# Gathering each 128-edge tile once a pass, with its visits reading a ring of tiles through registers

## The chip, the cores and the metric

One core of a Trainium2 chip runs the whole program. The metric is the device time of one execution in microseconds (us).

## The reference, cut to what matters

Three passes over the same 100,000 edges, sorted by destination node (6,250 nodes, 256 features). Each is an attention: a logit for each edge (and head), a softmax over the edges of a destination, and a weighted sum of the source rows.

```python
# layer 0, "gat": 4 heads of 64
logits = leaky_relu(a_src[src] + a_dst[dst], 0.2)
alpha  = segment_softmax(logits, dst)
x1     = segment_sum(h[src] * alpha[:, :, None], dst)
# layer 0, "attn": 1 head of 256
logits2 = einsum('ec,ec->e', q[d2], k[s2]) / sqrt(256)
out     = segment_sum(v[s2] * segment_softmax(logits2, d2)[:, None], d2)
# layer 1, "typed": 8 heads of 32, two edge types, a weight for each edge
alpha = leaky_relu(sum(xs_j * att_src[etype]) + sum(xd_i * att_dst[etype]))
out   = segment_sum(xs_j * (softmax over dst of alpha) * ew, dst)
```

Dense products, layer norms and a feed-forward stage stand between and behind the passes.

## The kernel before, in words

The edges lie in 782 tiles of 128. The nodes lie in 49 blocks of 128. A *visit* is one tile seen from one block: since edges are sorted, a tile that straddles two blocks has two visits, so there are at most 782 + 48 = 830 visits, padded to 832, in 52 batches of 16 (G). `edge_pass` runs once for each pass. Its engines each walk over the visits in a loop over v, and meet by semaphores alone:

- POOL (GpSimd, line 278) gathers the 128 source rows of a visit from a table in HBM by an indirect DMA, into one of 48 slots (gat, typed) or 40 (attn) of the ring X. It waits until the visit that had the slot is summed. The source numbers come from `tables`, which SP loads batch by batch; a tile with two visits is gathered twice.
- DVE (VectorE) makes the logits of a batch one batch ahead, at v = 16(k-1) for batch k. In gat and typed `source_logits` (line 466 or 469) adds the logit parts, which the gathered rows carry behind their 256 features, to those of the block. In attn `dot` (line 454) multiplies the gathered row with the expanded query, 25 visits ahead. A chain of scans (lines 515 to 566) takes the maxima of segments. Then `scale_rows` (line 591) multiplies each row by its weights in place, and `add` (line 613) adds the sum of the visit, which PE left in PSUM, to the block's accumulator. `blocks_of` (line 444) loads the 16 block numbers of a batch into DVE's registers.
- PE (TensorE) expands block values to edges (line 374 or 378), turns one-hot matrices (line 388), and sums a visit's rows by a matmul with the one-hot (line 425). `block_of` (line 356) loads four block numbers into PE's registers.
- ACT (ScalarE) copies the turned one-hots (line 334), takes exponentials (`weigh`, lines 287 to 299), in gat makes the transposed one-hots (lines 319, 326), in attn makes weighted one-hots (lines 307, 313).
- SP (SyncE) issues all other transfers of the pass (lines 227 to 250): tables, positions or one-hots, segments, joins, and in gat the stores of the one-hots.

```python
pool.wait_ge(S["summed"], v - RING + 1)                       # 277
pool.indirect_dma_start(X[:, v % RING, :], None, ph.table, ...)   # 278
row = X[:, v % RING, 0:D].rearrange("p (h c) -> p h c", h=H)
nc.vector.tensor_tensor(row, row, spread(row_weights[:, g, :], D // H), ALU.mult)   # 591
```

Of the kernel before, what the change touches and what calls it, by code (L numbers as in the profile page):

```python
# [23 lines left out]
PE_ENGINE = mybir.EngineType.PE  # L24

# [6 lines left out]
NT = (E + P - 1) // P  # L32
PAD_NODE = NP - 1
# [8 lines left out]
A = 6  # L42
SEG = 3 * P + 1
ARENA = 10400
BIG = 1e30
DST_SCALE = 1e30
FAR = 1000.0
H0, H2, FFN = 4, 8, 1024
W0 = D + 2 * H0
W1 = D + 4  # L50
# [81 lines left out]
class Phase:  # L132


    def __init__(self, m, name, heads, table, width, summed, keys, ring):
# [5 lines left out]
        self.ring = ring  # L141
        self.masked_at = {"gat": 2, "attn": 7, "typed": 3}[name]
        self.max_at = {"gat": 10, "attn": 13, "typed": 11}[name]
        self.X = m.big[:, 0:ring * width].rearrange("p (v w) -> p v w", w=width)
# [6 lines left out]
QUARTER = 4  # L151
# [5 lines left out]
def edge_pass(nc, m, dram, ph):  # L157

    H, R, X, K, RING = ph.H, ph.R, ph.X, ph.keys, ph.ring
# [38 lines left out]
    def onehot_t(k):  # L198

        return m.onehot_t[:, k % 2, :] if ph.dot else m.hot_ring.bitcast(BF16)[:, k % HOT, :]  # L200
# [3 lines left out]
    def rows_at(k):  # L204
        at = k * G % RING
        return X[:, at:at + G, :]

    with ExitStack() as ctx:
        S = Sems(nc, ctx, ph.name)
        block = ctx.enter_context(nc.Block())  # L210

        def landed(eng, v):
            eng.wait_ge(S[f"rows{v // QUARTER % groups}"], (v // RING + 1) * QUARTER * 16)

# [6 lines left out]
        def _(sp):  # L221
            def load_tables(k):
                if k >= TB:
                    if ph.dot:
                        sp.wait_ge(S["distance"], (k + 1 - TB) * G)
                    sp.wait_ge(S["dotted" if ph.dot else "scaled"], (k + 1 - TB) * G)
                sp.dma_start(m.tables[:, k % TB, :], dram.tables[k // (P // G), :, k % (P // G), :]).then_inc(S[f"tables{k % TB}"], 16)

            def load_onehots(k):
                if k >= hot:  # L230
                    if ph.dot:
                        sp.wait_ge(S["expanded"], (k - 1) * G)
                    else:
                        sp.wait_ge(S["onehots_turned"], (k + 1 - HOT) * 4)
                sp.dma_start(onehot_t(k), dram.onehot_t[k, :, :]).then_inc(S[f"onehot_t{k % hot}"], 16)

            def load_positions(k):
                if k >= 2:
                    sp.wait_ge(S["onehot_t"], k - 1)
                sp.dma_start(m.rel_row.bitcast(BF16)[:, k % 2, :], dram.rel16[k * G * P:(k + 1) * G * P].rearrange("(a n) -> a n", a=1).to_broadcast([P, G * P])).then_inc(S[f"positions{k % 2}"], 16)  # L240

            def store_onehots(k):
                sp.wait_ge(S["onehot_t"], k + 1)
# [1684 lines left out]
```

## Time and profile before

| what | value |
|---|---|
| time, median of 3 runs | 4141.51 us (4139.8 to 4142.21) |
| the profiled execution's own time | 4127.7 us |
| its span in the trace | 4126.1 us |
| gat pass: first gather issued, last addition of a visit starts | 141.74, 1217.66 us |
| attn pass: the same | 1384.24, 2452.04 us |
| typed pass: the same | 2626.68, 3705.24 us |
| gathers of each pass | 832 |
| mean time of one gather's issue | 946 to 948 ns |
| HBM read | 505.09 MB, mean 141 GB/s |

All that follows is read against the span of 4126.1 us. The profile's page names an engine's busy time and the idle time just before a group of instructions, with what ended it. Register, branch, semaphore and DMA-issuing instructions do not count as busy; idle time that ends with "issue" is time in which an engine waited for nothing that the profile shows.

### The profile page before, as it was taken

To read this page: it belongs to the slowest core of one execution; us is meant where nothing else is said; L and a number is where in the kernel's file an instruction comes from. 1 tells how busy PE (TensorE), PEld (TensorE's weight loads), DVE (VectorE), ACT (ScalarE), POOL (GpSimd) and SP (SyncE) were. 2 spreads that over 40 slices of the span, in tenths; PEclk is the share of its full clock that TensorE was granted. 3 is DMA by queue.
4 is the path that set the end of the run, shared out by engine and by line. 5 is a ranking of instruction groups with operands and counts; after the bars stand their busy time and mean duration, and the time that the engine had idled before them with its cause. 6 is when DMAs were issued, how large, how long until landed. Compare 5 with 4: busy or idle time off the path is not lost. (4 is left out here: it accounts for less than half of the span.)

```text
span 4126.1 us, 67495 instructions
## 1 busy us (share of the span) xinstructions
PE 3059.6 (74%) x15494; PEld 2152.1 (52%) x15494; DVE 3194.5 (77%) x11152; ACT 1535.4 (37%) x3947; POOL 2771.6 (67%) x3112
## 2 busy tenths in 40 slices
PE   6467677766667688778788779577777777768998
PEld 4344445444446455455555546344444444447887
DVE  6577888777787677777777769688888888887665
ACT  2333333333328466666666656211111111113332
POOL 3577777777730477777777745677777777746776
PEclk8778887788879799999999989788788888789999
DMA  7655555555534444444444436555555555532221
GB/s 144 176 168 166 167 167 168 170 173 168 167 82 131 137 136 140 139 137 137 137 137 137 139 96 221 186 157 159 156 157 156 156 159 160 152 85 89 66 66 46
DMA packets 297058, 586.64 MB, mean 142 GB/s; under 512 B 89485, under 2 KB 186777, under 8 KB 296746
## 3 DMA queue, kind: packets, MB, share of 16 engines
q0 software_dynamic: 123184, 355.57, 31.4%
q1 hardware_dynamic: 141434, 197.50, 16.0%
q10 hardware_dynamic: 32128, 29.99, 2.4%
q8 instruction: 126, 2.06, 0.2%
q14 instruction: 186, 1.52, 0.1%
HBM read 505.09 MB, written 77.73 MB: 141 GB/s over the span
## 5 line engine op out<-in xcount | busy, mean ns | idle before, releaser
L425 PE MATMUL psum<-big,onehots_or_distances 128*128 128x264 f32 (+2 forms) x4992 | 1885.5, 488 | 149.7 <-ACT onehots_or_distances L313 86.2
L613 DVE TENSOR_TENSOR acc<-acc,psum 128x264 f32 (+2 forms) x2496 | 1062.8, 426 | 259.1 <-PE psum L425 153.5
L425 PEld LDWEIGHTS psum<-big,onehots_or_distances 128*128 128x128 f32 x4992 | 937.1, 228 | 433.3 <-issue 167.7
L278 POOL DMA_INDIRECT big<-table_attn,tables x832 | 787.4, 946 | 453.8 <-DMA tables<-edge_tables 200.7
L278 POOL DMA_INDIRECT big<-table_typed,tables x832 | 788.7, 948 | 264.3 <-issue 194.6
L278 POOL DMA_INDIRECT big<-table_gat,tables x832 | 788.7, 948 | 263.7 <-issue 187.4
L334 ACT ACTIVATE onehots_or_distances<-psum 128x512 f32<-128x512 f32 x416 | 248.6, 597 | 1630.9 <-PE psum L388 1570.4
L591 DVE TENSOR_TENSOR big<-big,psum 128x256 f32<-128x256 f32 x1664 | 679.7, 414 | 26.9 <-ACT psum L299 1.4
L378 PE MATMUL psum<-big 128*128 x1664 | 279.4, 196 | 453.5 <-DVE raw L479 228.1
L374 PE MATMUL psum<-big,onehot_t 128*128 x2496 | 456.0, 294 | 113.9 <-DVE raw L454 102.0
L454 DVE CUSTOM_DVE_ANT_0 junk<-psum,big 128x258 f32<-128x258 f32 x832 | 346.2, 417 | 197.4 <-DMA big<-table_attn,tables 185.8
L378 PEld LDWEIGHTS psum<-big 128*128 128x128 bf16 x1664 | 187.3, 114 | 591.2 <-issue 520.7
L307 ACT ACTIVATE onehots_or_distances<-iota,tables 128x128 f32<-128x128 f32 x832 | 330.5, 397 | 386.7 <-DVE acc L613 376.8
L374 PEld LDWEIGHTS psum<-big,onehot_t 128*128 128x128 bf16 x2496 | 258.1, 104 | 305.4 <-issue 184.6
L313 ACT ACTIVATE onehots_or_distances<-onehots_or_distances,weight,neg_weight 128x128 f32<-128x128 f32 x832 | 397.6, 478 | 0.0
L388 PEld LDWEIGHTS psum<-ident,big 128*128 128x128 bf16 x1664 | 157.6, 116 | 102.9 <-issue 44.0
L1698 ACT ACTIVATE big<-psum,big 128x128 f32<-128x128 f32 x392 | 106.7, 383 | 258.2 <-PE psum L1737 258.2
L400 PE MATMUL psum<-growth,ones 64*128 64x4 f32 (+2 forms) x312 | 63.2, 272 | 180.5 <-DVE growth L566 180.5
L388 PE MATMUL psum<-ident,big 128*128 128x128 bf16 x1664 | 196.4, 252 | 0.0
L1737 PEld LDWEIGHTS psum<-big 128*128 128x128 f32 x1568 | 186.6, 195 | 5.9 <-ACT big L1690 3.4
L1737 PE MATMUL psum<-big 128*128 128x128 f32 x1568 | 187.1, 279 | 2.8 <-ACT big L1690 2.8
L773 POOL TENSOR_TENSOR big<-big,half 128x1 f32<-128x1 f32 x147 | 101.7, 692 | 117.5 <-DVE big L768 113.7
(265 smaller groups left out, 3959.8 us busy)
## 6 DMA issues: line engine op xcount, KB each, us to landing
big<-visit_positions SPq DMA_DIRECT2D x52, 512.0 KB
onehots<-big SPq DMA_DIRECT2D x52, 512.0 KB
onehot_t<-onehots SPq DMA_DIRECT2D x52, 512.0 KB
big<-onehots SPq DMA_DIRECT2D x52, 512.0 KB, 3.7
big<-table_gat,tables POOLq DMA_INDIRECT x832
big<-table_attn,tables POOLq DMA_INDIRECT x832
big<-table_typed,tables POOLq DMA_INDIRECT x832
big<-in_x_dram SPq DMA_DIRECT2D x98, 128.0 KB, 2.4
```

Source lines behind the costliest of these rows:

```text
L278: pool.indirect_dma_start(X[:, v % RING, :], None, ph.table, bass.IndirectOffsetOnAxis(ap=column(k, 0)[:, g:g + 1].bitcast(I32), axis=0)). ...
L307: nc.scalar.activation(m.dist[:, v % 4, :], m.iota[:, :], ACT.Abs, scale=-1.0, bias=column(k, 1)[:, g:g + 1]).then_inc(S["distance"], 1)
L313: nc.scalar.activation(m.onehots[:, v % 4, :], m.dist[:, v % 4, :], ACT.Relu, scale=m.neg_weight[:, k % 2, g:g + 1], bias=m.weight[:, k % ...
L334: nc.scalar.activation(m.onehots[:, at:at + 4, :], turned_onehots.rearrange("p (v n) -> p v n", n=P), ACT.Copy).then_inc(S["onehots"], 1)
L374: last = nc.tensor.matmul(ps[:, exp_banks[v % 3], 0:K], spreading, ph.tab[:, bass.ds(blk, 1), s, :].rearrange("p a k -> p (a k)"), start=( ...
L378: last = nc.tensor.matmul(expanded_at(g), spreading, ph.tab[:, bass.ds(blk, 1), :, :].rearrange("p a s k -> p (a s k)"), start=True, stop= ...
L388: last = nc.tensor.matmul(turned_onehots[:, i * P:(i + 1) * P], onehot_t(k)[:, g * P:(g + 1) * P], m.ident16[:, :], start=True, stop=True)
L425: nc.tensor.matmul(sum_ps(v), onehot_at(v), X[:, v % RING, 0:ph.WS], start=True, stop=True).then_inc(S["summed"], 1)
L454: nc.vector.tensor_tensor_reduce(out=m.junk[:, v % 3, 0:K], in0=ps[:, exp_banks[v % 3], 0:K], in1=X[:, v % RING, 0:K], scale=1.0, scalar=0 ...
L591: nc.vector.tensor_tensor(row, row, spread(row_weights[:, g, :], D // H), ALU.mult).then_inc(S["scaled"], 1)
L613: nc.vector.tensor_tensor(row, row, sum_ps(v), ALU.add).then_inc(S["added"], 1)
L1737: last = nc.tensor.matmul(ps[:, 2 + 2 * (p % 2) + f // 4, (f % 4) * P:(f % 4 + 1) * P], w1_t[:, c, f * P:(f + 1) * P], uT[:, p % 2, c * P: ...
```

## The change

A tile is gathered once. The ring X now holds 44 tiles in each pass, and a tile's slot is its number modulo 44. The number of slots is the same for all passes, and both visits of a straddling tile read the same slot. Which slot a visit reads is not known when the program is written, since it depends on the edges: the first stage computes, for each visit, its block and its slot, for each quarter of a batch the number of tiles that must have landed (`needs`), and for each quarter of tiles the last visit that reads it. These go through HBM to `m.index`, and the engines load them into registers. What each engine does differently in a pass:

- POOL waits once in four gathers (on `freed`), and reads the source numbers from `m.src`, loaded once for the whole program. It issues 782 gathers.
- SP only passes messages: for each four tiles it waits until they have landed and adds 4 to `arrived`; nine quarters later than a quarter it waits until that quarter's last visit is scaled (attn: summed), and adds 1 to `freed`. It loads one register for each.
- All other transfers of the pass are issued by ACT, at fixed steps of its loop.
- In gat and typed ACT copies the 4 or 16 logit parts of each visit's rows out of the ring (`copy_tails`, 16 small activations a batch), so that DVE can still add a batch's parts at once. It loads 16 slots and 4 needs a batch, and eight register steps test the needs' bounds.
- `scale_rows` reads X and writes to a second ring Y of 32 visits; the sums of gat and typed read Y. DVE loads 16 slots a batch.
- In attn `dot` is a scalar_tensor_tensor with an accumulated sum in place of the tensor_tensor_reduce; DVE loads 16 slots and 4 needs, and PE loads four slots each four visits for the sums.
- The gat table's rows are 260 numbers wide, not 264, the typed table's 272, not 288. `masked` and `type_one` wait for `tables`, on which POOL waited before.

The core of the diff:

```diff
+QUARTER = 4
-ARENA = 10400
+RING = 44
+YR = 2 * G
+LAG = 9
         @block.sync
         def _(sp):
+            for q in range(NTQ):
+                f = q - LAG
+                last = None
+                if 0 <= f < NTQ - groups:
+                    last = sp.value_load(m.index[64:65, f:f + 1], min_val=1, max_val=VISIT_END)
+                sp.wait_ge(S[f"rows{q % groups}"], 16 * (q // groups * QUARTER + min(QUARTER, NT - q * QUARTER)))
+                sp.sem_inc(S["arrived"], QUARTER)
+                if last is not None:
+                    sp.wait_ge(S["summed" if ph.dot else "scaled"], last)
+                    sp.sem_inc(S["freed"], 1)
         @block.gpsimd
         def _(pool):
-            for v in range(VISIT_END):
+            for t in range(NT):
+                if t >= RING and t % QUARTER == 0:
+                    pool.wait_ge(S["freed"], t // QUARTER - groups + 1)
+                pool.indirect_dma_start(X[:, t % RING, :], None, ph.table,
+                                        bass.IndirectOffsetOnAxis(ap=m.src[:, t:t + 1], axis=0))...
         @block.scalar
         def _(act):
+            def transfers(v):
+                for first_at, transfer in {"gat": [(9 - 5 * G, load_positions), (9 - 3 * G, store_onehots), (-2 * G, load_segments), (4 - 2 * G, load_tables)],
+                                           "attn": [(9 - 3 * G, load_onehots), (-2 * G, load_segments), (4 - 2 * G, load_tables)],
+                                           "typed": [(8 - 4 * G, load_onehots), (-2 * G, load_segments), (4 - 2 * G, load_tables)]}[ph.name]:
+            def copy_tails(v):
                 k, g = divmod(v, G)
+                if g == 0 and k >= 2:
+                    act.wait_ge(S["with_high"], k - 1)
+                if g % QUARTER == 0:
+                    act.wait_ge(S["arrived"], needs[g // QUARTER])
+                nc.scalar.activation(tails_at(k)[:, g, :], X[:, bass.ds(slots[g], 1), D:D + T]..., ACT.Copy)
...
+                u = v + 2 * G - 1
+                if not ph.dot and 0 <= u < VISIT_END:
+                    if u % G == 0:
+                        slots, needs = slots_of(ACT_ENGINE, u, G), needs_of(ACT_ENGINE, u // G)
+                    copy_tails(u)
         def _(pe):
-                    nc.tensor.matmul(sum_ps(v), onehot_at(v), X[:, v % RING, 0:ph.WS], start=True, stop=True)
+                    if ph.dot and v % 4 == 0:
+                        slots = slots_of(PE_ENGINE, v, 4)
+                    rows = tile_at(slots[v % 4], ph.WS) if ph.dot else Y[:, v % YR, :]
+                    nc.tensor.matmul(sum_ps(v), onehot_at(v), rows, start=True, stop=True)
         def _(dve):
-                for q in range(0, G, QUARTER):
-                    landed(dve, k * G + q)
+                dve.wait_ge(S["tails"], (k + 1) * G)
-                nc.vector.tensor_tensor(row, row, spread(row_weights[:, g, :], D // H), ALU.mult)
+                nc.vector.tensor_tensor(Y[:, v % YR, 0:D]..., row, spread(row_weights[:, g, :], D // H), ALU.mult)
+                u = v + (DOT_AHEAD if ph.dot else 1)
+                if 0 <= u < VISIT_END and u % G == 0:
+                    slots = slots_of(DVE_ENGINE, u, G)
+                    if ph.dot:
+                        needs = needs_of(DVE_ENGINE, u // G)
```

Where a slot is loaded in the stream of DVE in the typed pass, at the turn from one batch to the next. L613 (now L659) is the addition of a visit, L591 (L637) the scaling, L579 (L625) the scaling by edge weights, L466 (L510) the source logits; ISA is a register step. Before:

```order
L573 TENSOR_TENSOR shifted<-logit,psum 128x128
L613 ISA
L613 TENSOR_TENSOR acc<-acc,psum 128x272
L613 ISA
L613 TENSOR_TENSOR acc<-acc,psum 128x272
L579 TENSOR_TENSOR psum<-psum,tables 128x128
L591 TENSOR_TENSOR big<-big,psum 128x256 x2
L613 ISA
L613 TENSOR_TENSOR acc<-acc,psum 128x272
L591 TENSOR_TENSOR big<-big,psum 128x256
L466 TENSOR_TENSOR both<-big,psum 128x256
L444 TENSOR_LOAD blocks
```

The same place in the changed kernel:

```order
L659 ISA
L659 TENSOR_TENSOR acc<-acc,psum 128x272
L227 TENSOR_LOAD index
L625 TENSOR_TENSOR psum<-psum,tables 128x128
L637 ISA
L637 TENSOR_TENSOR big<-big,psum 128x256
L637 ISA
L637 TENSOR_TENSOR big<-big,psum 128x256
L659 ISA
L659 TENSOR_TENSOR acc<-acc,psum 128x272
L510 TENSOR_TENSOR dot_products<-dot_products,psum 128x256
L490 TENSOR_LOAD index
```

A load of 16 registers stands between the last addition of a batch and the first scaling of the next, beside the load of the block numbers (L444, now L490), and each scaling has a register step of its own.

In attn DVE has the loads behind the batch's masked logits (L549), ahead of a dot (L500):

```order
L659 TENSOR_TENSOR acc<-acc,psum 128x258
L549 TENSOR_TENSOR logit<-raw,tables 128x16
L227 TENSOR_LOAD index
L233 TENSOR_LOAD index
L233 ISA x8
L500 ISA
L500 SCALAR_TENSOR_TENSOR dot_products,raw<-psum,big 128x258
```

Two loads and eight register steps are new there. PE in the attn pass, at a visit that is a multiple of four; L471 is the sum, L417 the expansion, L399 the load of block numbers:

```order
L227 TENSOR_LOAD index
L471 ISA
L471 MATMUL psum<-big,onehots_or_distances 128x258
L417 ISA
L417 MATMUL psum<-big,onehot_t 128x258
```

A load and a register step now stand between the expansion and the sum, where the sum stood alone.

## Rows read from the trace of the kernel before

**Rows 1.** The page's head: span, busy time and share of each engine, instructions.

```profile
span 4126.1 us, 67495 instructions
...
PE 3059.6 (74%) x15494; PEld 2152.1 (52%) x15494; DVE 3194.5 (77%) x11152; ACT 1535.4 (37%) x3947; POOL 2771.6 (67%) x3112
```

**Rows 2.** The gathers' line: duration ns min/median/max, first and last start.

```profile
L278 POOL DMA_INDIRECT big<-table_gat,tables x832: 942/946/1105, 141.7 to 1182.6; - x167
L278 POOL DMA_INDIRECT big<-table_attn,tables x832: 942/946/1060, 1384.2 to 2423.9; - x167
L278 POOL DMA_INDIRECT big<-table_typed,tables x832: 942/946/1131, 2626.7 to 3667.6; - x167
```

**Rows 3.** POOL timeline, gat pass: start, us, idle before.

```profile
146.79 0.95 POOL L278 DMA_INDIRECT big<-table_gat,tables  x1 [0.30 <-issue]
148.04 0.95 POOL L278 DMA_INDIRECT big<-table_gat,tables  x1 [0.30 <-issue]
```

**Rows 4.** 100 us of each pass: busy us (instructions) of each engine.

```profile
core 0: us, PE busy (x) PEld busy (x) DVE busy (x) ACT busy (x) POOL busy (x), PEclk, DMA share, GB/s
500.00:600.00 100.00, 72.72 (x347) 50.07 (x348) 81.06 (x280) 33.45 (x45) 75.71 (x80) 0.81 0.57 169
1700.00:1800.00 100.00, 78.80 (x418) 51.00 (x417) 73.24 (x321) 61.44 (x173) 75.61 (x81) 0.95 0.49 138
3000.00:3100.00 100.00, 71.89 (x334) 47.07 (x333) 87.12 (x289) 15.32 (x35) 75.64 (x81) 0.83 0.56 158
```

**Rows 5.** DVE lines, gat, 300 to 1100 us: busy, mean ns, idle before.

```profile
L613 DVE TENSOR_TENSOR acc<-acc,psum 128x264 f32 x637 | 267.0, 419 | 93.2 <-PE psum L425 59.5 <-issue 28.5 <-DVE acc L613 1.7
...
L469 DVE TENSOR_TENSOR raw<-big,psum 128x64 f32<-128x64 f32 x40 | 10.4, 259 | 64.3 <-DMA big<-table_gat,tables 64.3
```

**Rows 6.** The same, attn pass, 1500 to 2300 us.

```profile
L454 DVE CUSTOM_DVE_ANT_0 junk<-psum,big 128x258 f32<-128x258 f32 x641 | 267.0, 417 | 146.7 <-DMA big<-table_attn,tables 140.6 <-PE psum L374 3.2
L613 DVE TENSOR_TENSOR acc<-acc,psum 128x258 f32 x641 | 266.2, 415 | 39.3 <-issue 19.3 <-PE psum L425 18.9
L454 DVE DVE_READ_ACCUMULATOR2_ANT raw<- 128x1 f32 x640 | 51.0, 80 | 0.0
```

**Rows 7.** The same, typed pass, 2750 to 3550 us.

```profile
L613 DVE TENSOR_TENSOR acc<-acc,psum 128x272 f32 x640 | 283.2, 443 | 66.6 <-PE psum L425 34.2 <-issue 29.6 <-DVE acc L613 0.4
...
L466 DVE TENSOR_TENSOR both<-big,psum 128x256 f32<-128x256 f32 x39 | 16.4, 421 | 24.7 <-DMA big<-table_typed,tables 24.3
```

**Rows 8.** Timeline of DVE, typed pass, at a batch's first visit.

```profile
3009.09 0.42 DVE L466 TENSOR_TENSOR both<-big,psum 128x256 f32<-128x256 f32 x1 [0.74 <-DMA big<-table_typed,tables]
3010.36 0.44 DVE L613 TENSOR_TENSOR acc<-acc,psum 128x272 f32 x1 [0.86 <-issue]
```

**Rows 9.** The lines that load registers: duration ns min/median/max.

```profile
L444 DVEq TENSOR_LOAD <-blocks x156: 1092/1099/2333, 183.4 to 3691.0; - x156
...
L356 PEldq TENSOR_LOAD <-blocks x624: 325/332/1832, 138.9 to 3661.8; - x156
```

**Rows 10.** The line of the sums' addition: the register step before it.

```profile
L613 DVEq FUSED_REGOPS  x2340: 57/57/57, 186.5 to 3705.1; - x195
```

**Rows 11.** Groups of PE lines, attn pass, 1500 to 2300 us.

```profile
L425 PE MATMUL psum<-big,onehots_or_distances 128*128 128x258 f32 x1282 | 435.9, 424 | 70.1 <-ACT onehots_or_distances L313 68.6 <-DVE raw L454 0.8
L374 PE MATMUL psum<-big,onehot_t 128*128 x1920 | 345.9, 289 | 71.3 <-DVE raw L454 69.0
```

**Rows 12.** Groups of ACT lines, gat pass, 300 to 1100 us.

```profile
L292 ACT ACTIVATE psum<-psum,first_hot 128x4 f32<-128x4 f32 x40 | 9.2, 230 | 0.0
```

**Rows 13.** Groups of ACT lines, attn pass, 1500 to 2300 us.

```profile
L307 ACT ACTIVATE onehots_or_distances<-iota,tables 128x128 f32<-128x128 f32 x641 | 254.6, 397 | 300.1 <-DVE acc L613 296.5
```

**Rows 14.** Timeline of SP and POOL at the start of the attn pass.

```profile
1382.16 0.81 SPq L227 DMA_DIRECT2D tables<-edge_tables  x2
1383.03 0.42 SPq L235 DMA_DIRECT2D onehot_t<-onehots  x1
...
1384.24 0.94 POOL L278 DMA_INDIRECT big<-table_attn,tables  x1 [200.66 <-DMA tables<-edge_tables]
```

More of the change, by code:

```diff
@@ L157, in edge_pass @@
 def edge_pass(nc, m, dram, ph):
-    H, R, X, K, RING = ph.H, ph.R, ph.X, ph.keys, ph.ring
+    H, R, X, Y, K, T = ph.H, ph.R, ph.X, ph.Y, ph.keys, ph.tails
     RQ = max(R, 32)
@@ L198, in onehot_t, with scaled_at, tails_at, tile_at @@
     def onehot_t(k):
-        return m.onehot_t[:, k % 2, :] if ph.dot else m.hot_ring.bitcast(BF16)[:, k % HOT, :]
+        if ph.dot or k % HOT >= 4:
+            return m.onehot_t[:, k % 2, :]
+        return m.hot_ring.bitcast(BF16)[:, k % HOT, :]
     turned_onehots = ps[:, 7, 0:4 * P]
-    def rows_at(k):
-        at = k * G % RING
-        return X[:, at:at + G, :]
+    def scaled_at(k):
+        return Y[:, k % 2 * G:(k % 2 + 1) * G, :]
+    def tails_at(k):
+        return m.tails[:, k % 2, :, 0:T]
+    def tile_at(slot, width):
+        return X[:, bass.ds(slot, 1), 0:width].rearrange("p a w -> p (a w)")
+    def slots_of(engine, v, n):
+        at = v // G * RECORD + v % G
+        return nc.values_load_multi_w_load_instructions(
+            m.index[32:33, at:at + n], engines=[engine], min_val=0, max_val=RING - 1,
+            skip_runtime_bounds_check_because="a tile's place in the ring is its number modulo the ring")[1]
+    def needs_of(engine, k):
+        at = k * RECORD + G
+        return nc.values_load_multi_w_load_instructions(m.index[32:33, at:at + 4], engines=[engine], min_val=1, max_val=NT)[1]
     with ExitStack() as ctx:
@@ L336, in _ @@
             weigh_at = G - 1 if ph.dot else G - 2
-            for v in range(-3 * G, VISIT_END):
+            slots = needs = ()
+            for v in range(-5 * G, VISIT_END):
+                transfers(v)
                 if ph.dot and 0 <= v + 1 < VISIT_END:
@@ L346, in _ @@
                     weigh(k)
[L347 removed]
+                if ph.name == "gat" and 0 <= v // G + 3 < NBATCH:
                     if v % G == 2:
@@ L778, in visits_and_nodes_in @@
     v_, n_ = Space(m.acc), Space(m.big[:, 0:16384])
-    rec = [v_.take(4 * P).bitcast(I32) for _ in range(VC)]
+    rec = [v_.take(3 * P).bitcast(I32) for _ in range(VC)]
     wrec = [v_.take(P) for _ in range(VC)]
@@ L790, in visits_and_nodes_in @@
     rel16 = [n_.take(P // 2).bitcast(BF16) for _ in range(2)]
-    scal = [n_.take(4) for _ in range(2)]
+    scal = [n_.take(3) for _ in range(2)]
     KB = NV // G
```

226 lines of the change are left out of this document (123 added, 103 removed).

## The prediction

> **What bounds the kernel now.** I read the head of the page first, for who is busy [rows 1]. No engine is above 77% of the span there, and that is the trap: the average hides three passes with one limit each. The next thing to read is the line of the gathers [rows 2]. In the gat pass 832 of them start between 141.7 and 1182.6 us, that is 1040.9 / 831 = 1.2526 us each; attn gives (2423.9 - 1384.2) / 831 = 1.2511 us, typed 1.2526 us. The timeline of POOL shows the same pitch from the first gathers on, when the ring is still empty and nothing can hold POOL back: 1.25 us, of which 0.95 is the issue and 0.30 a gap that no wait explains [rows 3]. So POOL issues at its own rate in all three passes, 81 gathers in each 100 us [rows 4], and the others follow. A batch of 16 visits takes 16 x 1.2526 = 20.04 us (attn 20.02).
>
> How much faster could the others go? That is what the lines of DVE tell, in a stretch of 800 us (39.9 batches) of each pass. DVE waits for gathered rows for 64.3 us in gat [rows 5], 140.6 us in attn [rows 6] and only 24.3 us in typed [rows 7]: 1.61, 3.52 and 0.61 us a batch. I take the batch less this wait as the pace that DVE and its partners could hold if the rows were always there: **18.43, 16.50 and 19.43 us**.
>
> **POOL's term.** It issues 782 gathers instead of 832. At 1.2526 us that is 979.5 us a pass, 18.84 us a batch, 62.6 us less a pass. Its width does not matter: 264, 260 and 288 numbers a row all take 946 ns in the median [rows 2]. That is all the change can give: 188 us. It is given only as far as the others come down to 18.84, and typed already stands at 19.43 without a single addition.
>
> **DVE's terms.** A load of 16 registers takes 1.10 us in the median [rows 9]. How much of it DVE feels is seen at a batch's first visit: the engine starts an instruction at 3009.09, and the next one only at 3010.36, 0.86 us idle with "issue" as the reason [rows 8]. The 40 gaps of this kind before the addition sum to 28.5 us in gat and 29.6 in typed, 0.71 and 0.74 a batch [rows 5, 7]. So DVE's sequencer is about one instruction ahead, which hides 0.3 us, and I price the new load of 16 slots at 0.8 us a batch. The bounds are 0 (it falls into a wait for PE, of which there are 34.2 us / 39.9 = 0.86 us a batch in typed [rows 7]) and 1.1. I do not take 0, because that wait ends with the addition ahead of the load, not with the scaling behind it. In attn a second load of 4 goes with it, 0.33 us by PE's row [rows 9], and eight register steps of 57 ns [rows 10], 0.46 us: 1.10 + 0.33 + 0.46 less 0.1 hidden behind a short instruction is 1.8 us. The added register steps of scalings and dots (57 ns) I price at nothing: an addition in front of a scaling runs 420 ns, and hides it; if that cover were gone it would be 16 x 0.057 = 0.9 us a batch, which I keep for the upper end. Scaling into Y instead of in place is the same shape, 0. The dot as scalar_tensor_tensor I price at 0 too: the one now takes 417 ns and an 80 ns read of the accumulator [rows 6], and the plain 258-wide addition in the same pass takes 415, so the width sets it; bounds -0.08 x 16 (no such read) and +0.1 x 16 us a batch.
>
> **PE's terms, attn.** Four loads of four slots a batch, 0.332 us each [rows 9], and 16 register steps stand between the wait for the one-hot and the sum: 1.3 + 0.9 = 2.2 us. PE is not the slowest, it waits 68.6 us / 39.9 = 1.7 us a batch for one-hots and as much for dots [rows 11]; but in the half of a batch without the chain of maxima DVE takes two instructions a visit and PE sets the pace. I take 0.9 us on the path, with bounds 0 and 2.2. What the Trainium skill says speaks for more: the page "DMA: Bandwidth & Descriptors", section "Latency and other measured facts", gives tensor_load a floor of about 600 ns. The trace of this kernel disagrees, with 624 loads at 332 ns in the median [rows 9]. By the page's figure PE's four loads would be an estimated 2.4 us a batch and attn would gain nearly nothing.
>
> **ACT's terms.** In gat ACT is busy about a third of the time [rows 4]. New in a batch: 16 tail copies at about 0.2 us (an activation of 4 columns takes 230 ns [rows 12]), 3.2 us; loads and bound tests, 1.10 + 0.33 + 0.46 = 1.9 us; five transfers at about 0.42 us [rows 14], 2.1 us. With today's 6.7 us (33.45% of 20.04) that is 13.9 us of 19. It fits, and I price it at nothing: what hides it is that ACT's copies serve visits 31 ahead. If the cover went, the first to feel it would be `source_logits`, behind two segment transfers and the last tail copy, and the one-hot copies (line 334) that PE waits for. In attn ACT has 61.4% and three to four transfers, 1.6 us, come in beside its activations; 0 again, it waits 296.5 us / 39.9 = 7.4 us a batch for additions [rows 13]. SP's relay delays an arrival by a few tenths and frees slots by quarters; POOL may be 40 to 44 tiles ahead and needs to be about 33, so 0.
>
> **The sum for each pass.** gat: max(18.84, 18.43 + 0.8) = 19.2 us a batch. attn: 16.50 + 1.8 + 0.9 = 19.2. typed: 19.43 + 0.8 = 20.2. The last two batches drain at the consumers' pace today as well, so I count 50 batches: gat 50 x (19.2 - 20.04) = **-42**, attn 50 x (19.2 - 20.02) = **-41**, typed 50 x (20.23 - 20.04) = **+10**.
>
> **At the ends.** POOL no longer waits for the first tables at a pass's start: SP's issue at 1382.16, POOL's at 1384.24 [rows 14], 2.1 us, three times: -6. The first 32 visits need about two gathers less (32 x 50 / 832), 2.5 us, three times, less relay and tail copies of about 1 us each (an estimate from the 0.2 us copies and semaphore steps): -3. The first stage gets a short chain of small DVE instructions and a round trip through HBM for the index, partly beside node work: +2, between 0 and 8. Together -7; the sum is -42 - 41 + 10 - 7 = **-80 us**, 4127.7 - 80 = 4047.7 for an execution like the profiled one. The median of the runs is 13.8 us above the profiled one, so for the median I say 4141.5 - 80 = **4061.5 us**. A measurement of this kernel can tell about 0.2%, 8 us.
>
> **Rivals.**
>
> *POOL stays the bound in all passes.* Then each gives 62.6 us: 4141.5 - 188 - 7 = 3946. For it: the typed batch has (66.6 + 24.7) / 39.9 = 2.3 us of DVE idle, which a new rhythm could use. Against it: most of that idle is register loads and waits for PE, not for rows [rows 7]. Chance 0.15.
>
> *ACT's stall comes onto the path, and it gets slower.* Place: the gat and typed passes, where ACT stands still for 1.9 us of loads a batch and only then copies tails, one-hots and weighs; DVE has no rows to scale until it has weighed. Price in full: 1.9 x 100 batches = +190, so 4061.5 + 190 = 4251. It decides once more than 80 / 100 = 0.8 us a batch of it is felt. For it: ACT's queue is in order and holds waits for arrivals and for DVE. Against it: the wait that ends the weighing comes 13 visits behind the loads. Chance 0.15.
>
> *Gains and losses cancel.* Attn's PE and DVE terms add up in full, 16.5 + 1.8 + 2.2 = 20.5, +24 instead of -41, and gat and the rest stay: 4126. Chance 0.08; within 0.2% a third of it, and some of the cases around it.
>
> *The register loads are dearer in the new places.* The longest load of 16 in the rows took 2.33 us against 1.10 [rows 9]. If all did, 1.23 x 50 x 3 = 185 us more: 4246. A page of the Trainium skill, "Runtime: NRT & Kernel Launch", section "Instruction fetch mechanics", gives about 200 ns a register even in bulk, which for 16 would be 3.2 us as an estimate and point the same way. The trace bears it out in none of its medians. Chance 0.02.
>
> **How the numbers follow.** My forecast has 0.6, for itself 4000 to 4120 (the bounds of the DVE and PE terms). With the first rival (3946) and the cancelling one (4126 and a little above) 0.83 lie between 3945 and 4150, which is the range. Faster: 0.6 + 0.15 and half of 0.08, less a bit for the forecast's upper tail, 0.77; same 0.06; slower 0.17.
>
> **What would show it.** POOL: 782 gathers at a pitch still 1.25 us where it runs free, but in typed and gat gaps every fourth one, ended by SP. DVE: no more wait for gathered rows in gat and typed; a second "issue" gap of 0.8 us a batch, before line 625 in typed or line 637 in gat. Typed is the pass that must not gain: if its batch goes below 19.6 us my DVE pace of 19.43 was wrong, since waits for PE were not intrinsic. If DVE waits for ACT's tails or weights by more than 0.5 us a batch, the second rival has come in.

## The result, and the profile after

The changed kernel is **slower**: 4191.06 us in the median (4187.99 to 4196.41, 4 runs) against 4141.86 (4139.8 to 4143.94, 4 runs) of the kernel before, a ratio of 1.012 with the 95% interval 1.0103 to 1.0136. The forecast was 4061.5 us, with a range from 3945 to 4150. The profiled execution has a span of 4194.4 us, 68.3 more than before.

The head of its page, beside [rows 1], and the line of the gathers, beside [rows 2] (duration ns min/median/max, first and last start):

```profile
span 4194.4 us, 78726 instructions
...
PE 3121.5 (74%) x15488; PEld 2165.3 (52%) x15488; DVE 3239.7 (77%) x11147; ACT 1740.4 (41%) x5611; POOL 2629.0 (63%) x2962
```

```profile
L262 POOL DMA_INDIRECT big<-table_gat,src_by_edge x782: 940/946/1118, 156.6 to 1186.3; - x196
L262 POOL DMA_INDIRECT big<-table_attn,src_by_edge x782: 940/946/1112, 1410.3 to 2422.4; - x196
L262 POOL DMA_INDIRECT big<-table_typed,src_by_edge x782: 940/946/1066, 2643.4 to 3713.1; - x196
its engine sat idle before it (us, times) until:
...
  SPq L255: 238.6, 197
```

The change does what it says, 782 gathers a pass. But in typed they now take from 2643.4 to 3713.1 us, 1.37 us each, and POOL waits 238.6 us, in the three passes together, for slots that SP frees. Here are 100 us of each pass, beside [rows 4]:

```profile
core 0: us, PE busy (x) PEld busy (x) DVE busy (x) ACT busy (x) POOL busy (x), PEclk, DMA share, GB/s
500.00:600.00 100.00, 70.59 (x340) 47.85 (x340) 79.66 (x273) 42.22 (x125) 71.94 (x76) 0.85 0.58 164
1700.00:1800.00 100.00, 81.86 (x422) 53.19 (x422) 76.77 (x329) 63.18 (x178) 75.64 (x81) 0.93 0.50 138
3000.00:3100.00 100.00, 74.56 (x323) 47.91 (x322) 85.25 (x281) 24.30 (x107) 68.44 (x73) 0.76 0.51 139
```

80 and 81 gathers became 76 in gat and 73 in typed, so POOL is no longer the bound there. DVE in typed runs 281 instructions in the 100 us where it ran 289: the consumers got slower. TensorE's granted clock (PEclk) in typed is 0.76 where it was 0.83, but that is not what slows DVE: its idle time before additions, where it waits for PE, fell from 66.6 us in [rows 7] to 52.1 in the rows below (the part put down to PE alone rose by 7). By stages, a pass being the time from its first gather to the start of its last addition:

| stage | before | after | change | forecast |
|---|---|---|---|---|
| up to the first gather | 141.7 | 156.6 | +14.9 | +2 |
| gat pass | 1075.9 | 1087.1 | +11.2 | -42 |
| between | 166.6 | 166.7 | +0.1 | 0 |
| attn pass | 1067.8 | 1060.5 | -7.3 | -41 |
| between | 174.6 | 172.6 | -2.1 | 0 |
| typed pass | 1078.6 | 1129.4 | +50.8 | +10 |
| end | 420.8 | 421.6 | +0.8 | 0 |

(The forecast's other -9 us lie at the passes' starts.) The lines of DVE say where, over 800 us of gat, attn and typed, beside [rows 5], [rows 6] and [rows 7]:

```profile
L659 DVE TENSOR_TENSOR acc<-acc,psum 128x264 f32 x635 | 264.6, 417 | 76.0 <-PE psum L471 65.9 <-issue 4.5 <-DVE acc L659 1.9
L637 DVE TENSOR_TENSOR big<-big,psum 128x256 f32<-128x256 f32 x636 | 261.7, 417 | 80.5 <-DVE acc L659 34.2 <-ACT psum L331 2.8 <-issue 2.2
L513 DVE TENSOR_TENSOR raw<-dot_products,psum 128x64 f32<-128x64 f32 x40 | 10.2, 254 | 0.0
```

```profile
L500 DVE SCALAR_TENSOR_TENSOR dot_products<-psum,big 128x258 f32<-128x258 f32 x643 | 269.6, 419 | 112.6 <-issue 78.5 <-SPq L252 28.2 <-PE psum L417 4.1
L659 DVE TENSOR_TENSOR acc<-acc,psum 128x258 f32 x643 | 267.7, 416 | 57.8 <-issue 27.9 <-PE psum L471 26.9
```

```profile
L659 DVE TENSOR_TENSOR acc<-acc,psum 128x272 f32 x610 | 268.3, 440 | 52.1 <-PE psum L471 41.6 <-issue 6.7 <-DVE acc L659 3.2
L637 DVE TENSOR_TENSOR big<-big,psum 128x256 f32<-128x256 f32 x610 | 251.4, 417 | 41.0 <-issue 0.7
...
L625 DVE TENSOR_TENSOR psum<-psum,tables 128x128 f32<-128x128 f32 x38 | 11.4, 299 | 27.9 <-issue 27.9
```

In gat no wait for gathered rows is left (L513 has 0.0 where the kernel before had 64.3). In its place DVE stands idle for 80.5 us before the *scaling* (L637), and the largest named part of that ended with the addition ahead of it on the same engine. It shows best in a timeline, first of the kernel before, then of the changed one (start, us):

```profile
3696.06 0.43 DVE L613 TENSOR_TENSOR acc<-acc,psum 128x272 f32 x1
3696.53 0.42 DVE L591 TENSOR_TENSOR big<-big,psum 128x256 f32<-128x256 f32 x1
```

```profile
3099.99 0.43 DVE L659 TENSOR_TENSOR acc<-acc,psum 128x272 f32 x1
3100.56 0.42 DVE L637 TENSOR_TENSOR big<-big,psum 128x256 f32<-128x256 f32 x1
...
3102.94 0.44 DVE L659 TENSOR_TENSOR acc<-acc,psum 128x272 f32 x1 [1.11 <-PE psum L471]
3104.11 0.30 DVE L625 TENSOR_TENSOR psum<-psum,tables 128x128 f32<-128x128 f32 x1 [0.73 <-issue]
```

**From the start of an addition to the start of the scaling right behind it 0.47 us became 0.57.** The pair is typical: in the median of all 318 such pairs of typed it was 0.47 and is 0.57, and in the 420 of gat 0.46 and 0.56. An idle stretch that short is seldom put down to a cause, which is why the waits' totals hide it. The last two rows are the load of 16 slots: 0.73 us with nothing to do, priced at 0.8.

Why 0.10 more? A scaling waits until the addition ahead of it has ended (line 589 before, `added` >= v - 3). In the stream of DVE that wait stood on the scaling. Now a register step (ISA) comes first and carries it. In this listing of the instruction stream the first line is the kernel before, the next two are the changed one. The name in brackets is that of a semaphore of the first stage, whose number `added` uses again:

```
L591 TENSOR_TENSOR big<-big,psum 128x256 [waits first_row_stored0]

L637 ISA [waits first_row_stored0]
L637 TENSOR_TENSOR big<-big,psum 128x256
```

In the timeline above the addition of 3099.99 ends at 3100.42, the step starts at 3100.46, 57 ns long, and the scaling at 3100.56.

### The profile page after: what moved, and what is told of

It reads as the page before. It is cut to its first block and busy times, and to the rows that moved or that the text cites. A ratio compares the mean times of both kernels' runs of the same rounds, so it can differ in the third digit from the quotient of the medians.

```text
span 4194.4 us, 78726 instructions
## 1 busy us (share of the span) xinstructions
PE 3121.5 (74%) x15488; PEld 2165.3 (52%) x15488; DVE 3239.7 (77%) x11147; ACT 1740.4 (41%) x5611; POOL 2629.0 (63%) x2962
## 5 line engine op out<-in xcount | busy, mean ns | idle before, releaser
L471 PE MATMUL psum<-big,onehots_or_distances 128*128 128x264 f32 (+2 forms) x4992 | 1937.1, 496 | 296.7 <-ACT onehots_or_distances L345 117.2
L471 PEld LDWEIGHTS psum<-big,onehots_or_distances 128*128 128x128 f32 x4992 | 936.8, 229 | 631.8 <-issue 485.1
L659 DVE TENSOR_TENSOR acc<-acc,psum 128x264 f32 (+2 forms) x2496 | 1059.0, 424 | 247.8 <-PE psum L471 177.3
L262 POOL DMA_INDIRECT big<-table_attn,src_by_edge x782 | 740.7, 947 | 495.4 <-issue 225.4
L262 POOL DMA_INDIRECT big<-table_typed,src_by_edge x782 | 740.8, 947 | 341.4 <-issue 213.2
L262 POOL DMA_INDIRECT big<-table_gat,src_by_edge x782 | 740.5, 947 | 301.1 <-issue 215.1
L637 DVE TENSOR_TENSOR big<-big,psum 128x256 f32<-128x256 f32 x1664 | 685.2, 417 | 171.4 <-DVE acc L659 40.3
L417 PE MATMUL psum<-big,onehot_t 128*128 x2496 | 442.0, 288 | 79.2 <-DVE dot_products L500 67.8
L500 DVE SCALAR_TENSOR_TENSOR dot_products<-psum,big 128x258 f32<-128x258 f32 x832 | 348.4, 419 | 149.4 <-issue 101.8
L313 ACT ACTIVATE dot_products<-big 128x4 f32 (+1 forms) x1664 | 250.8, 202 | 404.0 <-issue 302.4
L417 PEld LDWEIGHTS psum<-big,onehot_t 128*128 128x128 bf16 x2496 | 253.0, 101 | 252.1 <-issue 130.0
L421 PE MATMUL psum<-big 128*128 x1152 | 194.8, 196 | 239.3 <-DVE dot_products L520 107.9
L421 PEld LDWEIGHTS psum<-big 128*128 128x128 bf16 x1152 | 130.3, 115 | 335.7 <-issue 290.3
L443 PEld LDWEIGHTS psum<-growth,ones 64*128 64x128 f32 (+2 forms) x312 | 49.8, 199 | 262.3 <-DVE growth L612 262.3
L1822 PE MATMUL psum<-big 128*128 128x256 f32 x784 | 177.2, 379 | 0.0
```

Of the source, the lines that this page charges most:

```text
L262: pool.indirect_dma_start(X[:, t % RING, :], None, ph.table, bass.IndirectOffsetOnAxis(ap=m.src[:, t:t + 1], axis=0)).then_inc(S[f"rows{t ...
L313: nc.scalar.activation(tails_at(k)[:, g, :], X[:, bass.ds(slots[g], 1), D:D + T].rearrange("p a w -> p (a w)"), ACT.Copy).then_inc(S["tail ...
L417: last = nc.tensor.matmul(ps[:, exp_banks[v % 3], 0:K], spreading, ph.tab[:, bass.ds(blk, 1), s, :].rearrange("p a k -> p (a k)"), start=( ...
L421: last = nc.tensor.matmul(expanded_at(g), spreading, ph.tab[:, bass.ds(blk, 1), :, :].rearrange("p a s k -> p (a s k)"), start=True, stop= ...
L471: nc.tensor.matmul(sum_ps(v), onehot_at(v), rows, start=True, stop=True).then_inc(S["summed"], 1)
L500: nc.vector.scalar_tensor_tensor(m.junk[:, v % 3, 0:K], ps[:, exp_banks[v % 3], 0:K], 1.0, tile_at(slots[v % G], K), ALU.mult, ALU.mult, a ...
```

## The experiments

Three theories. **T1:** the scaling's register step stands behind the wait for the addition, so its 57 ns and the start of the scaling come after the addition's end, some 15 times a batch; with the slots' load this makes DVE the bound of gat and typed. **T2:** ScalarE, with its new loads, tail copies and transfers, is late with the weights. **T3:** SyncE's relay of messages and the freeing of slots by quarters hold POOL back.

The runs form five groups, each with the kernel before beside it. In groups 2, 3 and 5 that kernel took 4129.3 to 4130.25 us, and their totals can be set side by side. In groups 1 and 4 it took 4780.07 and 4735.43 us; the last section tells of these. The passes, in us, and the median of the whole:

| run | group | gat | attn | typed | median | ratio (95%) |
|---|---|---|---|---|---|---|
| a0, changed kernel again | 2 | 1082.9 | 1064.1 | 1127.6 | 4183.57 | 1.0127 (1.011 to 1.0143) |
| e1, wait moved | 2 | 1035.0 | 1060.6 | 1046.0 | 4045.75 | 0.9785 (0.9764 to 0.9806) |
| e4, moved and loads split | 2 | 1050.9 | 1062.4 | 1043.2 | 4068.55 | 0.9857 (0.9838 to 0.9875) |
| e6, all | 2 | 1035.0 | 1037.8 | 1037.4 | 4023.38 | 0.9741 (0.9725 to 0.9757) |
| e3, fixed rows (no steps, no slot loads) | 3 | 1023.5 | 1062.3 | 1038.2 | 4036.03 | 0.9774 (0.9758 to 0.979) |
| e8, the same program as e3 | 3 | 1028.4 | 1058.6 | 1034.0 | 4036.74 | 0.9777 (0.9761 to 0.9794) |
| e2, loads split alone | 3 | 1106.6 | 1065.6 | 1153.5 | 4237.46 | 1.0258 (1.0241 to 1.0275) |
| e7, ScalarE light | 3 | 1086.2 | 1061.4 | 1118.5 | 4180.93 | 1.0132 (1.0114 to 1.0149) |
| c2, steps and loads in the kernel before | 5 | 1101.0 | 1069.1 | 1135.3 | 4213.89 | 1.0208 (1.0187 to 1.0228) |
| e10, best | 5 | 1028.9 | 1045.8 | 1040.5 | 4018.97 | 0.973 (0.9714 to 0.9747) |

**The wait moved.** The addition waits for its predecessor itself, PE waits for the bank of sums in gat too, and the scaling, whose step stays, waits for neither.

```diff
 def scale_rows(v):
-                if v >= 4:
-                    dve.wait_ge(S["added"], v - 3)
 def add(v, blk):
-                elif ph.dot or v >= VISIT_END - 3 or v % G == G - 3:
+                else:
                     dve.wait_ge(S["added"], v)
 # TensorE
-                    if v >= SB and (ph.typed or v == VISIT_END - 1):
+                    if v >= SB and (not ph.dot or v == VISIT_END - 1):
                         pe.wait_ge(S["added"], v + 1 - SB)
```

> The scaling's wait for the preceding addition goes to the next addition and, in gat, to the sum on TensorE; the register step is left. T1 (the 57 ns register step of a scaling stands behind that wait, so it runs only after the addition has ended: 0.10 us more for some 15 scalings a batch, 1.5 us a batch in gat and typed): gat falls from 20.0 to the gathers' 18.8 us a batch (-60 us), typed from 20.8 to 19.4 (-77 us), attn stays; about 4055 us in all. T2 (ScalarE's register loads, tail copies and transfers make the weights late): within 10 us of 4191. T3 (the ring comes free too late because SP passes it on by quarters): within 10 us of 4191.

Its first run is in group 1: 5162 us against 4780. The time from addition to scaling is down to 0.34 us all the same, but the total says nothing without the changed kernel beside it. So both ran again in group 2. The first of the two expectations also names a fourth theory, T4, about group 1:

> The changed kernel as it is, beside the others on one chip, because the kernel before took 4780 us on the chip of the first four runs and not 4142. If the chip is as the first one: 1.2% over the kernel before. If it is as the second one, where TensorE and the engines behind it wait up to 5 us at a time for nothing that the profile shows: T4 (a longer instruction stream is what this chip is slow at: 78726 instructions against 67495) says 5 to 8% over the kernel before.

> The move of the scaling's wait alone, beside the changed kernel. In the first run of it the step from an addition to the scaling behind it fell from 0.57 to 0.34 us, as T1 has it, but the total could not be read without the changed kernel beside it. T1: on a chip like the first one 100 to 140 us less than the changed kernel (ratio to the kernel before 0.98); on the slow one, where DVE waits for TensorE anyway, under 30 us less. T2 and T3: within 10 us of the changed kernel.

Timeline of DVE in gat, moved wait, second run:

```profile
518.74 0.42 DVE L657 TENSOR_TENSOR acc<-acc,psum 128x264 f32 x1
519.08 0.41 DVE L635 TENSOR_TENSOR big<-big,psum 128x256 f32<-128x256 f32 x1
```

It is 0.34 us for the pair, and 138 us less than the changed kernel in the same group: 48 in gat, 82 in typed, 4 in attn. POOL is back at its own pace in 100 us of each of the two passes:

```profile
700.00:800.00 100.00, 74.75 (x360) 50.71 (x357) 80.88 (x290) 44.45 (x134) 75.52 (x81) 0.83 0.60 171
...
3000.00:3100.00 100.00, 73.16 (x350) 47.41 (x348) 88.16 (x301) 27.02 (x117) 75.62 (x81) 0.86 0.56 153
```

T2 and T3 allowed 10 us: ScalarE's and SyncE's work is unchanged here. They fall as the main cause; POOL's waits for SP went from 238.6 to 78.7 us with SP's program as it was. But here the pair became shorter than in the kernel before, so this run alone doesn't tell whether the wait costs by itself or only with the step behind it.

**No step, the wait left.** The scalings of gat and typed read constants at a fixed place, so this kernel leaves the gathered rows out of these two passes' sums.

```diff
-                row = tile_at(slots[g], D).rearrange("p (h c) -> p h c", h=H)
+                row = m.iota[:, 0:D // H].unsqueeze(1).to_broadcast([P, H, D // H])
```

> The scalings of gat and typed multiply fixed constants instead of the gathered row and have no register step (left out: the gathered rows in those two passes' sums); the wait for the preceding addition, the slots' loads and the gathers stay. T1: 0.11 us less for some 15 scalings a batch: typed from 20.8 to 19.1 us a batch (-85 us), gat from 19.9 to the gathers' 19.0 (-48 us); about 4050 us, within 20 us of the run with the wait moved. If the wait alone were the cost and not the step behind it: within 10 us of the changed kernel's 4184.

The pair is at 0.45 us again, as before the change (gat, second run):

```profile
521.35 0.42 DVE L659 TENSOR_TENSOR acc<-acc,psum 128x264 f32 x1
521.80 0.42 DVE L637 TENSOR_TENSOR big<-iota,psum 128x256 f32<-128x256 f32 x1
```

So the wait alone costs nothing that was not there before; with the step behind it, it does. Against a0, gat and typed fall by 59.4 and 89.4 us. But not all of that is the steps'. The expectation says that the slots' loads stay, and the trace says otherwise: nothing reads these registers any more, and of DVE's loads of 16 slots (the changed kernel, then e3) only attn's 52 are left.

```profile
L227 DVEq TENSOR_LOAD <-index x156: 1095/1100/1360, 191.1 to 3754.1; - x156
```

```profile
L227 DVEq TENSOR_LOAD <-index x52: 1095/1100/1110, 1349.8 to 2355.7; - x52
```

So e3 takes away steps and loads together. Their shares can be read from the gaps between DVE's instructions, a0 less e3, from a pass's first to its last addition. In typed the gaps before scalings shrink by 61 us and the gap before line 625, where the load stands, by 27. The 61 are 34 at the 318 scalings right behind an addition, and 27 at 459 others, which stand behind a mostly shorter instruction. In gat the load's gap, before a batch's first scaling, shrinks by 28 us and the gaps before the other scalings by 60, and other waits take back 27. T1's count was therefore wrong: only 6 to 8 scalings of a batch stand right behind an addition, and that 15 x 0.115 comes to typed's 1.72 us a batch is luck.

**And no slot loads.** Here the source drops the loads too, which e3's program had already lost.

> As the run before, and VectorE's load of 16 slots of a batch is left out too in gat and typed (nothing reads them). T1: the load's 0.74 us of idle VectorE a batch goes wherever VectorE is still the bound: typed to the gathers' 18.9 to 19.0 (-5 to -15 us against the run before), gat unchanged: 4035 to 4050 us.

Both programs have 76958 instructions, 1768 fewer than the changed kernel: 1664 steps and 104 loads. So this run is e3 once more and tests nothing new. It does show how much a pass differs from execution to execution: typed is 4 us lower, gat 5 higher, the whole the same. What the load costs where DVE has room is seen in e1, which keeps it: typed takes 8 to 12 us more there than in e3 and e8, steps and loads together.

**The register half alone, put into the kernel before.** It keeps its 832 gathers, fixed places and static output. DVE loads 16 registers with zeros once a batch in gat and typed, and a scaling adds one of them to the address that it reads. (The cut leaves out the load.)

```diff
+                read = X[:, v % RING, bass.ds(zeros[g], D)].rearrange("p (h c) -> p h c", h=H)
-                nc.vector.tensor_tensor(row, row, spread(row_weights[:, g, :], D // H), ALU.mult)
+                nc.vector.tensor_tensor(row, read, spread(row_weights[:, g, :], D // H), ALU.mult)
```

> The kernel before with the register half of the change alone (VectorE's loads of 16 registers a batch and a register step at each scaling of gat and typed, which carries its wait; all gathers and static places as before). Its first run fell on a chip where the kernel before took 4735 us and VectorE waited for TensorE. On a chip like the first, T1: typed 20.8 us a batch instead of 19.9 (+47 us), gat 20.0 instead of 19.8 (+8 us): about 4185 us. T2, T3: within 10 us of 4130.

It took 4213.89, 85 us more than the kernel before in that group; the expectation had 55. Set beside the table of stages, typed carries 57 of it (1135.3 against 1078.6), gat 25, attn 1. Most of the excess is in gat, where 8 were expected: the load of 16 took 1.53 us there in the mean, up to 2.93, against 1.10 in typed. The pair, in gat:

```profile
519.83 0.42 DVE L615 TENSOR_TENSOR acc<-acc,psum 128x264 f32 x1
520.39 0.42 DVE L593 TENSOR_TENSOR big<-big,psum 128x256 f32<-128x256 f32 x1
```

It is 0.56 us, with none of the shared places, relays or ScalarE work. **Steps that carry the wait, and the slots' loads, are the loss.** All the rest of the change, the fewer gathers among it, makes it 30 us smaller (a0's 4183.57). No run has the steps without the loads, since a step needs a loaded register; their shares rest on the gaps read above.

**The converse:** the kernel before with its wait moved as in e1, where nothing should come of it.

> The kernel before with the same move of the wait. Its passes run at the pace of the gathers (1.2526 us each), and its scalings have no register step: within 5 us of 4142 by all theories. A gain of over 20 us would mean that the wait costs without the step too.

It took 4772.14 against 4780.07 (ratio 0.9987, 0.9977 to 0.9997), 8 us where 5 were allowed, and again 4732.2 against 4735.43 in group 4 (0.9992, 0.9982 to 1.0001). Both are groups of the longer time, so that it gains nothing where the kernel before takes 4130 us isn't shown.

**ScalarE light.** ScalarE loads no slots and copies its tails from constants, so the gathered logit parts are left out.

```diff
-                        slots, needs = slots_of(ACT_ENGINE, u, G), needs_of(ACT_ENGINE, u // G)
+                        needs = needs_of(ACT_ENGINE, u // G)
-                nc.scalar.activation(tails_at(k)[:, g, :], X[:, bass.ds(slots[g], 1), D:D + T]..., ACT.Copy)
+                nc.scalar.activation(tails_at(k)[:, g, :], m.iota[:, 0:T], ACT.Copy)
```

> ScalarE in gat and typed loads no slots (1.19 us a batch) and copies its tails from constants, without a register step (left out: the gathered tails in the logits of these passes); its waits for gathers and its transfers stay. T2: the weights come earlier, up to 1.2 us a batch in both passes: 60 to 120 us less than the changed kernel's 4184. T1: VectorE stays the bound: within 10 us of 4184.

It took 4180.93, T1's answer: against a0 3 us more in gat, 9 less in typed, 3 less in all. T2 falls.

**Small loads instead of one large: a miss of mine, twice.** The 16 slots as four times 4, first with the wait moved:

```diff
+                if g % 4 == 0:
+                    slots = slots_of(DVE_ENGINE, v, 4)
-                row = tile_at(slots[g], D).rearrange("p (h c) -> p h c", h=H)
+                row = tile_at(slots[g % 4], D).rearrange("p (h c) -> p h c", h=H)
```

> Wait moved, and VectorE's 16 slots of a batch loaded in gat and typed as four times 4. T1: in typed another 0.7 us a batch (-38 us), in gat little more, since the gathers' 18.84 us a batch is reached already (0 to -20 us): 140 to 190 us less than the changed kernel, ratio 0.97. T2 and T3: within 10 us of the changed kernel.

Against e1, typed gained 3 us, which is no more than two executions differ by, and gat lost 16. In typed there was little left to gain: the gathers start over 990.5 us, 1.27 each. In gat the loads are sometimes slow (line of the loads, 250 to 1100 us of gat, then 2700 to 3600 of typed; duration ns min/median/max), and one falls into the chain of maxima:

```profile
L227 DVEq TENSOR_LOAD <-index x173: 337/343/1781, 255.6 to 1095.9; - x173
```

```profile
L227 DVEq TENSOR_LOAD <-index x187: 342/346/362, 2704.1 to 3599.4; - x187
```

```profile
505.75 0.14 DVE L607 TENSOR_TENSOR grown<-joined_t 64x1 f32<-64x1 f32 x1
506.70 0.42 DVE L640 TENSOR_TENSOR big<-big,psum 128x256 f32<-128x256 f32 x1 [0.81 <-issue]
```

Of the 208 loads in gat 41 took over 0.6 us, each of them 1 to 2 us after ScalarE issued a batch's store of one-hots (at 503.59 here). Then the split without the moved wait:

> The changed kernel with VectorE's 16 slots loaded as four times 4 in gat and typed, the wait where it was. With the wait moved the split gave nothing in typed and cost 15.7 us in gat, where 41 of 206 such loads took 0.8 to 1.8 us instead of 0.34, all of them 1 to 2 us after the issue of a batch's one-hot store. T1: typed, where VectorE is the bound here, falls by up to 0.7 us a batch (-20 to -38 us); gat gains 0.7 and loses the same by the slow loads (-20 to +20 us): 4125 to 4185 us. T2: within 10 us of 4184.

It took 4237.46: slower by 54 us than a0, where I had said faster or equal. Timeline of DVE in typed:

```profile
3116.55 0.43 DVE L664 TENSOR_TENSOR acc<-acc,psum 128x272 f32 x1
3117.50 0.42 DVE L642 TENSOR_TENSOR big<-big,psum 128x256 f32<-128x256 f32 x1 [0.52 <-DVE acc L664]
```

The 0.57 us between the two are 0.95 here. The stream says why: a load that comes first inherits the wait.

```
L227 TENSOR_LOAD index [waits first_row_stored0]
L642 ISA
L642 TENSOR_TENSOR big<-big,psum 128x256
```

It is T1's mechanism with a load of 344 ns in front of the step of 57. A rival is that a load costs its time wherever it stands. Against it: the same loads cost typed nothing in e4, where no wait is in front of them.

**Attn and the combined versions.** e6 adds to e4: attn's slots in fours, its bounds of arrived gathers one at a time, the block numbers in fours, and SyncE's last loads of x ahead of the index.

> As the run before, and besides: the slots of attn and the blocks of all passes loaded by VectorE as four times 4, one bound of arrived gathers at a time in attn, and in the first stage SyncE's last loads of x ahead of the round trip of the index. T1: attn falls from 19.9 us a batch to the gathers' 18.84 or what TensorE allows, 19.2 (-35 us), typed by another 0.7 us (-36), the first stage by 12: some 70 us less than the run before, ratio 0.955 on a chip like the first.

Attn fell by 25 us against e4, and e6 took 4023.38. Which of its parts gained in attn was to be told by e9, with slots and bounds alone; it is in group 4 (5069 against 4735), without the changed kernel beside it, so this is open.

> The changed kernel with attn's part alone edited on VectorE: 16 slots of a batch as four times 4, and the four bounds of arrived gathers, read and tested together, one at a time between two visits. With the blocks split too attn took 997 us from first to last addition instead of 1021 to 1024. T1: most of that comes from these two: attn 19.7 to 19.3 us a batch (-20 us), the other passes as they were: about 4165 us. If it came from the blocks: no change.

The last version, e10, is e6 with the slots of gat and typed loaded 16 at a time again:

> The wait moved, blocks and attn's slots in fours, bounds one at a time, the last loads of x ahead of the index; gat's and typed's slots 16 at a time. On a chip like the first, T1: gat 18.9 to 19.0 us a batch, attn 19.2, typed 19.1 to 19.2: 4005 to 4025 us, ratio 0.972. On one like the last, 8 to 9% over the kernel before, as in its first run.

e10 takes 4018.97 us, 2.7% under the kernel before. Gat is 6 us under e6, as it should be with no small loads near the store, but attn is 8 above with the same code, so a difference of 5 us in the total says nothing. Whether the later index helps is not decided: the first gather came at 142.3 us in e6 but at 148.5 in e10, and the changed kernel had 149.0 (a0) and 156.6.

## Why the prediction was wrong

**The step that failed** is in DVE's terms: "The added register steps of scalings and dots (57 ns) I price at nothing: an addition in front of a scaling runs 420 ns, and hides it". The length of the cover was right. What was missed is that the step can't start under it, since the wait for that very addition goes to whichever instruction of the scaling comes first. What it cost in typed, by the gaps before scalings: 61 us, 1.18 us a batch, over the 0.9 that was kept as the bound for lost cover. With the slots' load it comes to 89 us in typed and 59 in gat, together 149. The wait stands in the code (line 589), but [rows 5] and [rows 7] have no group for it, since it costs too little there.

What the Trainium skill says fits: the page "Perfetto Trace Analysis", section "Per-engine timelines", has a DVE instruction pushed into a wait queue, the sequencer going on to decode the next, while an instruction of the sequencer itself holds the sequencer through its wait. The trace agrees: a scaling with the wait on itself starts 0.45 to 0.47 us after the addition, one whose step has the wait 0.56 to 0.57, one whose step has none 0.34.

**POOL's term** (18.84 us a batch where nothing else binds) was right: gat with no steps and loads (e3) and with the wait moved (e1) takes 1023.5 and 1035.0, -52 and -41 against the -42 forecast.

**DVE's pace in typed** (19.43 us without waits for rows) was too slow. Typed in e3 runs from first to last addition in 991.3 us, 19.06 a batch, and in e1, steps and loads included, in 999.1, 19.21, under the 19.6 that the prediction named as the sign. In the changed kernel itself this error is hidden by the larger one: 19.06, the steps' 1.18 and the load's 0.52 make 20.76, and 20.82 was measured (1082.5 / 52).

**The slot load** was priced at 0.8. The idle time is 0.73, and a0 less e3 gives it 0.52 us a batch in typed. As a term on top of any pace it was the wrong account: in e1 the same idle time stands before line 625, and typed is 8 to 12 us from the runs without it.

**Attn** was to gain 41 and gained 7. The loads and tests make 78.5 us of "issue" before the dots, 1.97 us a batch against 1.8 (the eight steps of the bound tests take 0.84 us, four of 186 and four of 23 ns, and not eight times 57), and waits for arrivals 28.2 us, 0.7 a batch, which were priced at zero. Idle time before additions rose from 39.3 to 57.8 us, 0.46 a batch, where PE's term was 0.9. Together with 16.50 that is 19.6, which is what attn took (1020.9 / 52). Also, -41 was counted against 20.02 us a batch, while from first to last addition the kernel before takes 1028.9 / 52 = 19.79: it starts late behind the gathers and catches up. That overstated each pass by some 10 us.

**The first stage** took 14.9 us more, in a second execution 7.2, against +2 with a bound of 8. That is not explained.

**The second rival** had the sign, by the wrong engine: e7 clears ScalarE.

## What to carry to other kernels

A dynamic address puts a register step in front of an instruction, and that step, or a register load ahead of it, takes over the instruction's waits: where it waits for the instruction just ahead on its own engine, nothing hides it. Put such a wait on something later (here the next addition) before adding the register. Price a step by who carries the wait, not by its length beside its neighbour's; and when work is taken from a bound engine, recount the next one with all its own small steps, since here steps and register loads cost 149 us in the two passes where the saved gathers could give 125. And before reading a variant that leaves something out, count its instructions in the trace: what nothing reads may be gone too, as e3's loads were.

## What the runs showed of the hardware

- A load of registers from SBUF takes DVE 344 ns for 4 and 1100 for 16 in the median, so 63 ns a register and some 90 fixed. The Trainium skill, page "Runtime: NRT & Kernel Launch", section "Instruction fetch mechanics", has about 200 ns a register; no run here shows that.
- The same load of 4 takes up to 1.78 us when it falls 1 to 2 us behind the issue of a 512 KB store from SBUF, in gat only (41 of 208 in e4, none of typed's 208). Why is not shown.
- **The five groups.** In groups 1 and 4 the passes alone took longer; the end took 421 to 423 us everywhere. The granted clock of the kernel before was 0.80 there against 0.86, in the mean of the execution; whether that is cause or consequence is not shown. Against groups 2, 3 and 5 it took 15 to 16% longer, c2 13%, and those of the changed kernel's variants that ran in both 20 to 28%:

| run | group | instructions | median | ratio |
|---|---|---|---|---|
| c1, before, wait moved | 1 | 69516 | 4772.14 | 0.9987 |
| c1, before, wait moved | 4 | 69516 | 4732.2 | 0.9992 |
| c2, before, steps and loads | 4 | 69264 | 4762.24 | 1.0051 |
| e3, fixed rows | 1 | 76958 | 5050.07 | 1.0578 |
| e9, changed, attn's loads | 4 | 79038 | 5069.08 | 1.0696 |
| e2, loads split | 1 | 79038 | 5098.35 | 1.0684 |
| e10, best | 4 | 81527 | 5147.75 | 1.0866 |
| e1, wait moved | 1 | 80747 | 5162.24 | 1.0803 |

The order by length is roughly T4's, but c1 has 2021 instructions more than the kernel before (67495) and costs nothing, and c2, with 1769 more, costs 0.5%, so it is not length as such. There an engine starts long after the work that it waits for. In e9 DVE waits for PE's transpose, whose record ends at 187.93, and starts at 203.93:

```profile
187.59 0.34 PE L448 MATMUL psum<-ident,seg_max 64*128 64x64 f32 x1
...
203.93 0.23 DVE L622 TENSOR_TENSOR big<-psum,tables 128x64 f32<-128x64 f32 x1 [17.74 <-remote]
```

The trace has the rise of the semaphore that the transpose raises at 203.91, so DVE itself starts at once, and it is the report of PE's work that comes 16 us late. A register step of ScalarE took up to 1387 ns there, where the changed kernel's took 60 at most (line of the tail copies, e9, then the changed kernel):

```profile
L317 ACTq FUSED_REGOPS  x1664: 9/55/1387, 163.0 to 4609.6; - x185
```

```profile
L313 ACTq FUSED_REGOPS  x1664: 55/55/60, 169.9 to 3733.6; - x185
```

One gather's issue took 946 to 956 ns in the mean there, almost as ever. What holds the engines there is open. It bears on the verdict: the version that wins by 2.7% where the kernel before takes 4130 us loses 8.7% where it takes 4735.
